# A ViT layer on one core: the residual's upper 128 channels summed on GpSimd, and pieces of three queues in another order

## The reference, cut to what matters

```python
h = einsum(patches(x), W) + b                                   # 576 tokens x 192
h = layernorm(h + attention(h))                                 # 12 heads of 64
# feed-forward of 8 experts, the two best of each token, weighted
logits = h @ Wr + br;  topk_vals, topk_idx = top_k(logits, 2);  scores = softmax(topk_vals)
gu = minimum(h @ Wgu[e] + bgu[e], 7);  gate, up = gu[:192], maximum(gu[192:], -7)
act = (up + 1) * gate * sigmoid(1.702 * gate)
out = layernorm(h + sum_e score_e * (act @ Wd[e] + bd[e]))
```

## Time and profile before

| | |
|---|---|
| median of 3 runs | 141.36 us (141.29 to 142.15) |
| the profiled execution | 141.29 us |
| its span, first to last instruction | 139.4 us |
| granted TensorE clock, mean | 0.997 |
| busy: PE, PEld, DVE, ACT, POOL | 131.2, 122.3, 97.6, 77.6, 78.6 us |

### The profile page before, as it was taken

One profiled execution on the slowest core, in us unless ns is written; L12 is line 12 of the kernel. 1 busy time (PEld: TensorE's weight loads), 2 busy tenths in 40 slices (PEclk: granted clock), 3 DMA queues, 4 the chain that ended last, 5 costly groups with the idle time before them and its releaser, 6 DMA issues. The chain is left out here.

```text
span 139.4 us, 4023 instructions
## 1 busy us (share of the span) xinstructions
PE 131.2 (94%) x1585; PEld 122.3 (88%) x1586; DVE 97.6 (70%) x254; ACT 77.6 (56%) x150; POOL 78.6 (56%) x90
## 2 busy tenths in 40 slices
PE   6999899999999999996999999999998999999960
PEld 2779899999898889996989999999998989999940
DVE  0129589648959877646578687887798886688743
ACT  3057789989852557588468433144223455443671
POOL 7402158780478998999852863399552444244500
PEclk9999999999999999999999999999999999999998
DMA  4999964630122223322840000000000000000022
GB/s 133 302 375 405 413 218 121 219 113 0 28 56 54 69 68 93 127 81 78 296 167 0 0 0 7 0 0 0 0 5 0 0 0 0 7 0 2 0 65 62
DMA packets 5962, 12.42 MB, mean 89 GB/s; under 512 B 888, under 2 KB 2872, under 8 KB 5944
## 3 DMA queue, kind: packets, MB, share of 16 engines
q1 hardware_dynamic: 5944, 12.18, 25.8%
HBM read 9.96 MB, written 0.44 MB: 75 GB/s over the span
## 5 line engine op out<-in xcount | busy, mean ns | idle before, releaser
L476 POOL TENSOR_TENSOR reg_r<-reg_p,reg_r 128x324 fp32r<-128x324 f32 (+1 forms) x23 | 19.4, 843 | 21.9 <-ACT reg_r L708 21.9
L708 ACT ACTIVATE reg_r<-reg_p 128x324 fp32r<-128x324 f32 (+1 forms) x24 | 10.7, 444 | 29.0 <-DVE reg_p L1067 29.0
L408 POOL TENSOR_TENSOR reg_w<-stage,reg_w 128x768 fp32r<-128x768 f32 x12 | 22.6, 1887 | 5.2 <-ACT reg_w L540 5.2
L1271 PE MATMUL ps<-reg_r,reg_w 128*128 128x324 f32 (+1 forms) x48 | 14.8, 308 | 0.0
L1067 DVE SCALAR_TENSOR_TENSOR reg_p<-reg_q 128x324 f32<-128x324 f32 (+1 forms) x24 | 13.2, 552 | 2.2
L1044 DVE TENSOR_SCALAR reg_q<-ps,bup 128x324 f32<-128x324 f32 (+1 forms) x24 | 12.3, 511 | 3.1 <-PE ps L1275 3.0
L1272 PE MATMUL ps<-reg_r,reg_w 128*128 128x324 f32 (+1 forms) x48 | 14.2, 296 | 0.0
L1275 PE MATMUL ps<-reg_r,reg_w 128*128 128x324 f32 (+1 forms) x48 | 14.2, 295 | 0.0
L1273 PE MATMUL ps<-reg_r,reg_w 128*128 128x324 f32 (+1 forms) x48 | 14.2, 295 | 0.0
L1274 PE MATMUL ps<-reg_r,reg_w 128*128 128x324 f32 (+1 forms) x48 | 14.1, 295 | 0.0
L446 POOL TENSOR_TENSOR reg_q<-reg_q,rnorm 128x432 f32<-128x432 f32 x7 | 8.9, 1276 | 6.4 <-ACT rnorm L618 6.4
(11 more groups left out here) (196 smaller groups left out, 391.6 us busy)
## 6 DMA issues: line engine op xcount, KB each, us to landing
reg_x<-xw_in SPq DMA_DIRECT2D x5, 416.0 KB, 6.0
stage<-w_gu_a SPq DMA_DIRECT2D x4, 384.0 KB, 4.3
stage<-w_gu_b SPq DMA_DIRECT2D x4, 384.0 KB, 3.3
reg_r<-reg_x SPq DMA_DIRECT2D x24, 54.0 KB
stage<-w_qkv_a SPq DMA_DIRECT2D x3, 384.0 KB, 7.6
stage<-w_qkv_b SPq DMA_DIRECT2D x3, 384.0 KB, 8.0
stage<-w_down SPq DMA_DIRECT2D x3, 384.0 KB, 4.7
wout<-w_out SPq DMA_DIRECT2D x1, 576.0 KB, 9.6
```

Source lines behind the costliest of these rows:

```text
L408: nc.gpsimd.tensor_tensor(dst[:, 1, :], raw, f(dst[:, 0, :]), ALU.subtract).then_inc(s_wlop, 1)
L476: nc.gpsimd.tensor_tensor(acts[:, n % NACT, 1, 0:w], act_f[:, n % 4, 0:w], f(acts[:, n % NACT, 0, 0:w]), ALU.subtract).then_inc(s_alo, 1)
L1271: mm(out_ap, w_a(0), x[:, 0, cols], start=True, stop=False)
```

## The change

It does four things. (1) Residual: the identity matmuls of channels 0 to 127 (L1538, L1539) go, the bias matmul L1541 starts the bank, and a new step on GpSimd, `residual_sum(a)`, adds hi and lo into `hsum` (which lies in reg_x), after act_lo(9) and after act_lo(13). (2) Evacuation: ACC goes to zT on VectorE as a sum with hsum (`z_main`), ACC + 1 on ScalarE (`z_tail`), for part 1 in two pieces of 126 columns each, and the transposes wait piece by piece; z_main(0) stands ahead of expert_act(13) in VectorE's list. (3) act_hi(23) moves from ScalarE, where it stood behind the table load, to VectorE. (4) GpSimd's order of the weight pieces 10 to 16.

```diff
+        hsum = reg_x[:, 0:0 + T]
...
+        def z_parts(a):
+
+            return [slice(0, TS[0])] if a == 0 else [slice(ZS[1] * i, ZS[1] * i + ZS[1]) for i in range(ZN[1])]
...
+            def residual_sum(a):
+
+                pool.wait_ge(s_h1lo, (6, 2 * NTT)[a])
+                pool.wait_ge(s_pv, NU)
+                cols = slice(TO[a], TO[a] + TS[a])
+                nc.gpsimd.tensor_tensor(hsum[:, cols], f(h1T[:, 0, cols]), f(h1T[:, 2, cols]), ALU.add).then_inc(s_hsum, 1)
...
                 if k in (3, 5, 6):
-                    w_lo({3: 7, 5: 9, 6: 11}[k])
+                    w_lo({3: 7, 5: 9, 6: 10}[k])
                 probs(k)
...
-                if k == 5:
-                    w_lo(10)
             root(2, TSIZES[2], s_ve, s_rstd)
-            w_lo(12)
+            w_lo(11)
             gap_exp(0)
             gap_exp(1)
             gap_exp(2)
             pool.wait_ge(s_w2, 6)
+            w_lo(12)
+            root(3, TSIZES[3], s_ve, s_rstd)
             w_lo(13)
-            root(3, TSIZES[3], s_ve, s_rstd)
-            w_lo(14)
             act_lo(0)
             act_lo(1)
             act_lo(2)
             root(4, TSIZES[4], s_ve, s_rstd)
             act_lo(3)
+            w_lo(14)
+            act_lo(4)
             w_lo(15)
-            act_lo(4)
+            act_lo(5)
             w_lo_full(16)
-            act_lo(5)
+            act_lo(6)
             w_lo_tail(16)
-            act_lo(6)
             gap_exp(3)
             gap_exp(4)
             for n in range(7, LAST_LO):
                 act_lo(n)
+                if n in (9, NT + 1):
+                    residual_sum(n // NT)
...
-            def z_copy(a):
+            def z_tail(a):
 
                 act.wait_ge(s_dn, NT * (a + 1))
                 if a == 1:
                     act.wait_ge(s_zt, 1)
-                nc.scalar.activation(zT[:, 0, 0:TS[a]], ps[:, ACC, 0:TS[a]], ACT.Copy).then_inc(s_z, 1)
+                for cols in z_parts(a):
+                    nc.scalar.activation(zT[:, 1, cols], ps[:, ACC + 1, cols], ACT.Copy).then_inc(s_zd, 1)
...
-                act_hi(n if n >= NT + 4 else n - 1)
+                if n < 2 * NT - 1:
+                    act_hi(n if n >= NT + 4 else n - 1)
                 if n == 11:
                     w2_hi(1)
                 if n == NT + 2:
-                    z_copy(0)
+                    z_tail(0)
...
-            z_copy(1)
+            z_tail(1)
...
+            def act_hi(n):
+
+                dve.wait_ge(s_act, n + 1)
+                dve.wait_ge(s_ahi, n)
+                dve.wait_ge(s_dn, n - NACT + 1)
+                w = TS[n // NT]
+                nc.vector.tensor_copy(acts[:, n % NACT, 0, 0:w], act_f[:, n % 4, 0:w]).then_inc(s_ahi, 1)
...
-            def z_tail(a):
+            def z_main(a):
 
                 dve.wait_ge(s_dn, NT * (a + 1))
+                dve.wait_ge(s_hsum, a + 1)
                 if a == 1:
                     dve.wait_ge(s_zt, 1)
-                nc.vector.tensor_copy(zT[:, 1, 0:TS[a]], ps[:, ACC + 1, 0:TS[a]]).then_inc(s_zd, 1)
+                for cols in z_parts(a):
+                    nc.vector.tensor_tensor(zT[:, 0, cols], ps[:, ACC, cols], hsum[:, TO[a] + cols.start:TO[a] + cols.stop],
+                                            ALU.add).then_inc(s_z, 1)
...
                     weigh(n - 1)
+                    if n == NT + 2:
+                        z_main(0)
                     expert_act(n - 1)
...
-                if n == NT + 2:
-                    z_tail(0)
...
+            act_hi(2 * NT - 1)
             act_lo(2 * NT - 1)
-            z_tail(1)
+            z_main(1)
...
-                mm(ps[:, ACC, 0:w], ident_r[:, :], h1T[:, 0, cols], start=True, stop=False, skip_group_check=True)
-                mm(ps[:, ACC, 0:w], ident_r[:, :], h1T[:, 2, cols], start=False, stop=False, skip_group_check=True)
                 mm(ps[:, ACC + 1, 0:w], ident_r[:, :], h1T[:, 1, cols], start=True, stop=False, skip_group_check=True)
-                mm(ps[:, ACC, 0:w], bd[:, 0:DA], w2T[:, cols], start=False, stop=False, skip_group_check=True)
+                mm(ps[:, ACC, 0:w], bd[:, 0:DA], w2T[:, cols], start=True, stop=False, skip_group_check=True)
...
-                pe.wait_ge(s_z, a + 1)
-                pe.wait_ge(s_zd, a + 1)
...
+                    pe.wait_ge(s_z, 2 + i if a else 1)
                     nc.tensor.transpose(ps[0:n, b, o:o + DA], zT[:, 0, tok], ident[:, :])
+                    pe.wait_ge(s_zd, 2 + i if a else 1)
```

More of the change, by code:

```diff
@@ L219, in vit_layer @@
          s_gm, s_um, s_bm, s_glu, s_u, s_b, s_act, s_ahi, s_alo, s_alod, s_dn, s_z, s_zd, s_zt, s_zs,
-         s_zst, s_zmv, s_zve, s_zrstd, s_znb, s_zln, s_zr1, s_res) = [
+         s_zst, s_zmv, s_zve, s_zrstd, s_znb, s_zln, s_zr1, s_res, s_hsum) = [
             sem(n) for n in (
@@ L227, in vit_layer @@
                 "s_gm s_um s_bm s_glu s_u s_b s_act s_ahi s_alo s_alod s_dn s_z s_zd s_zt s_zs "
-                "s_zst s_zmv s_zve s_zrstd s_znb s_zln s_zr1 s_res").split()]
+                "s_zst s_zmv s_zve s_zrstd s_znb s_zln s_zr1 s_res s_hsum").split()]
         pieces = []
```

## The result

In 22 runs each, on the same chips and side by side, the kernel before took 141.63 us (median) and the changed one 142.06 us: a ratio of 1.0043 [1.0029, 1.0058], 0.4% slower. Its `var_e` of tile 1, the input of root(1) and the row at which the first change of order begins to count, starts at 62.98, in the earlier trace rows at 62.20; over all profiles here it lies between 62.12 and 63.11, whichever order of GpSimd is in force, and in every profile project(1) starts 3.00 to 3.01 ahead of it. So I compare *aligned*: the span less the start of that row.

What follows compares the result with a forecast made beforehand. It took TensorE's matmul stream, between its few waits, as the kernel's clock. Terms of +0.65 (w_lo(14), net of earlier gains), +0.09 (residual(1)) and -0.40 (tail) made +0.34 on 141.29, so 141.6 us, range 139.8 to 142.7.

Steps and rivals of the forecast that it cites:

- Root(1) ahead of w_lo(10): On GpSimd: root(1) no longer queues behind w_lo(10), so ln1(1) and project(2) start earlier, by 1.05 us.
- The replaced wait: Rival at project(2): another wait takes the place of the removed one, all 1.05 us lost; 142.7 us, chance 0.15.
- Residual(0): On TensorE: two matmuls fewer take 0.30 us out, but project(4) also waits for h1_lo(3), so 0.08 us is kept.
- w_lo(14) in the queue: GpSimd, act_lo(3) to gap_exp(3): one more piece adds 1.78 us, leaving router_weights(3) and spread(10) 0.65 us late.
- residual(1): z_main(0) ahead of expert_act(13) delays ScalarE's copy by 0.32 us; less two matmuls, spread(15) comes 0.09 us later.
- The tail: At the end: act_hi(23) on VectorE gains 0.32 us, the evacuation in halves 0.08, together 0.40 us.
- The sums on GpSimd: Two additions, 0.88 us for the wider, each lie in one of GpSimd's waits for ScalarE and cost nothing.
- The rival of the missed holds: Rival: shifted VectorE and GpSimd pairs miss each other, saving four holds of 0.28 us; 140.5 us, chance 0.20.
- The kept gain: Rival: GpSimd's queue does not decide, so the 1.13 us gained ahead of w_lo(14) stays; 139.85 us, chance 0.18.

Runs made afterwards that it cites:

- kernel 10: The kernel before with only the changed kernel's early GpSimd order, w_lo(14) staying ahead of act_lo(0); 140.78 us beside 141.66, ratio 0.9942.
- kernel 1: The kernel before with GpSimd's whole new order of pieces alone; 142.38 us beside 141.50, ratio 1.0074.
- Kernel 6: The changed kernel with z_main(0) behind expert_act(13) instead of ahead of it; 142.02 us beside 141.72, ratio 1.002.
- Kernel 7: The changed kernel with act_hi(23) back on ScalarE behind the table load; 142.17 us beside 141.66, ratio 1.0059.
- kernel 3: The changed kernel with w_lo(14) moved one place up, ahead of act_lo(3); 141.78 us beside 141.50, ratio 1.0034.
- kernel 5: The changed kernel with w_lo(14) ahead of act_lo(0), w_lo(15) staying behind act_lo(4); 141.52 us beside 141.72, ratio 1.0005.
- kernel 4: The changed kernel with gap_exp(3) ahead of act_lo(6) and w_lo_tail(16); 140.69 us beside 141.50, ratio 0.9948.
- kernel 8: The changed kernel with w_lo(14) ahead of act_lo(0) and GpSimd's old order from act_lo(3) on; 140.49 us beside 141.72, ratio 0.9917.
- kernel 9: As kernel 8, with gap_exp(3) also ahead of w_lo_tail(16) and act_lo(6); 140.70 us beside 141.72, ratio 0.9946.
- kernel 11: As kernel 9, with z_main(0) also behind expert_act(13); 140.26 us beside 141.66, ratio 0.991.
- kernel 12: The same kernel as kernel 8, run again; 141.07 us beside 141.66, ratio 0.9927.

## Why the prediction was right, by its steps

The forecast of 141.6 us was +0.34 on its base; the aligned traces show +0.42, the medians +0.43. The mechanism came as told. That the sum is so close is in part luck: the terms were off by +0.14, -0.07 and -0.03 us, with another 0.04 behind the transposes. The terms, one by one:

- *Root(1) ahead of w_lo(10)*, -1.05 forecast: 1.10 at gate_up(0), and kernel 10 carries -1.01 to the end. The replaced wait did not come.
- *Residual(0)*, -0.08: nothing of it. Project(4) waited for h1_lo(3), as the text had feared, and act_lo(3) was 1.01 ahead, not 1.13.
- *w_lo(14) in the queue*, 1.78 of queue for +0.65 net: the queue grew by 1.82 (10.54 against 8.72), kernels 1 and 10 differ by 1.76, and net it was +0.79 at spread(10). The missing 0.14 is mainly the 0.12 that act_lo(3) had not gained. This is the term that decided the sign.
- *residual(1)*, +0.09: aligned, spread(15) is 0.02 later relative to spread(10). Kernel 6 confirms that z_main(0) ahead of expert_act(13) costs the order of 0.1.
- *The tail*, -0.40: down(23)'s last matmul 0.34 earlier relative to spread(15), the copies 0.09 shorter. Kernel 7 gives 0.28 for act_hi(23) by itself.
- *The sums on GpSimd*, nothing: nothing in time, but not as told. The first took 1.15 us, not 0.88, and did not fit the wait for ScalarE: act_lo(10) stands right behind it and comes 0.12 late behind act_lo(9). The second (116.61, 0.72 us) held expert_act(14) to 0.95 us, where it took 0.42, and act_lo(14) comes 0.33 later behind act_lo(13). TensorE waits for neither.

One reading was wrong without effect: TensorE's waits have more than four places, and the longest is not the 1.05 us before project(2) but 1.3 us for `reg_h` (L1237), at the very start of the span, where the change touches nothing and which the changed kernel has too. One detail was wrong in a direction that mattered later. The text had router_weights(3) idle for some 1.9 us (its own terms, 0.44 + 1.78, make 2.2), and it idled 1.14. VectorE had got there late itself, because two expert_acts took 0.6 us longer each than in the kernel before. What failed there is the size of a hold: "these two engines hold each other up by some 0.28 us each time" was read off the rows of the GpSimd side, and VectorE's side was left at what it showed in a stretch where no expert_act happened to begin early in a long piece. The sentence behind it, that an L1067 inside the piece is held to its end, was right, and so was the reason why it cost nothing here: VectorE waited for gap_exp(3) all the same. In kernels 3 and 5, where the queue was relieved, the same holds took the whole gain. The Trainium skill has this as a rule that I had not weighed (SBUF — State Buffer, section Who interferes with whom): a VectorE instruction with two SBUF inputs contends with a GpSimd instruction that reads SBUF, because its second input comes through the read interface that the two share, and the shared ports are an exclusive lock. The runs agree for the long GpSimd instructions: 0.50 us became 2.02, ending 0.36 us behind the piece. Beside the single-column gap_exp(3) of kernel 4 no hold shows: there expert_act took its 0.50 us and ended 0.09 us behind it.

The rival of the missed holds priced the right thing with the wrong sign: shifted by a piece, the pairs did not miss each other but met at longer ones. The kept gain (139.85, that is -1.44) is what kernels 8, 9, 11 and 12 show to be there once the piece stands elsewhere: aligned -1.4.

## What to carry to other kernels

Read the slack of a queue at the place where its next waited-for result stands, not over the whole: GpSimd had 2.35 us of idle time just ahead of act_lo(3), and one piece behind it cost 1.8 us. When the instructions of two engines hold each other up, ask of every long step which short instruction of the other engine will begin inside it; moving a piece of 1.8 us, and the two steps of the next, by one place, with the same work, was worth 0.8% here. And when a wait is gone, look whether the instruction ahead of it is held in its place, before counting the gain.

## What the runs showed that was not expected

*The hold has the length of the other engine's rest.* An expert_act of 324 columns that is held ends 0.34 to 0.36 us after the GpSimd instruction in whose span it began, at all five places shown above (gap_exp(3) of kernel 4 held none). So its length depends on where it begins: up to 1.16 us in an act_lo, up to 2.02 in a piece of 768 columns. Weigh, whose second input is in PSUM, stays at 0.40 to 0.49 in all profiles. The GpSimd operation next in line pays too: an act_lo of 324 columns right behind such a meeting takes 1.12 to 1.18 us instead of 0.88.

*A cast from SBUF to SBUF is cheap.* Act_hi(23) on VectorE took 0.29 us for 252 columns, where ScalarE takes 0.41 and the forecast had allowed 0.42. GpSimd was idle at that time. A cast can be held too: in kernel 4 one of two columns (L1027, 98.96), begun inside act_lo(6), took 0.57 us, ending 0.03 us behind it, where it takes 0.15 in the changed kernel.

*TensorE's clock fell in a stretch in which the engine was busy.* In the profiled executions of kernels 8 and 12, which are the same kernel, the granted clock was 0.50 (the 1.2 GHz level) from about 70.3 to 73.6 us, and in that of kernel 3 from about 70.2 to 80.4. Here are the windows of kernel 12: in each the busy time of the engines, then the granted clock, the DMA share and GB/s.

```profile
69.00:70.00 1.00, 1.00 (x50) 0.86 (x50) 0.60 (x5) 0.35 (x1) 0.83 (x1) 1.00 0.98 316
70.00:71.00 1.00, 1.00 (x16) 0.96 (x8) 0.80 (x5) 0.53 (x1) 0.20 (x1) 0.63 0.84 326
71.00:72.00 1.00, 1.00 (x6) 1.00 (x6) 0.41 (x3) 0.85 (x2) 0.35 (x1) 0.50 0.98 382
72.00:73.00 1.00, 1.00 (x5) 1.00 (x5) 0.84 (x8) 1.00 (x2) 0.55 (x1) 0.50 0.05 18
73.00:74.00 1.00, 1.00 (x6) 0.86 (x4) 0.93 (x8) 0.15 (x1) 0.18 (x1) 0.66 0.00 0
```

TensorE shows no idle time in any of them. In the 2 us before the fall it ran small matmuls, of 8 to 108 columns; behind it the first matmuls of gate_up(0) came 0.27 us apart, in kernel 11 0.15. From project(2) to project(3) kernel 12 took 12.21 us and kernel 11, with the same instructions up to there, 10.64. The difference is the 1.57 us used above. Why it fell in these executions and not in those of kernels 9, 10 and 11, whose TensorE ran the same matmuls before it, is open; no run was made for it.
